# A GNN block on one core: the first columns of the adjacency built gather by gather, x loaded in three requests, a body of 80 first units

## The chip, the cores and the metric

The kernel runs on one core of a Trainium2 chip. The metric is the device time of one execution in microseconds (us).

## The reference

There are N = 1250 nodes with 512 features, and 21250 edges that come sorted by `dst`; each node has a loop edge. Two graph layers follow each other.

```python
agg = jax.ops.segment_sum(x[src], dst, num_segments=N)      # A^T x, A counts the edges
h = (1.0 + eps) * x + agg
h = relu(batch_norm(h @ W1 + b1, g1, be1))                   # 512 -> 1024
h = relu(batch_norm(h @ W2 + b2, g2, be2))                   # 1024 -> 512
x = layernorm(x + x + h)
h = relu(x @ lW1 + lb1) @ lW2 + lb2                          # 512 -> 256 -> 512
x = layernorm(x + h + segment_sum(h[src], dst, N))
```

## The kernel before

The sparse sum is turned into dense products. The kernel builds the count matrix AT (source nodes in 10 row tiles `k` of 128, destination nodes as 1250 columns) and multiplies x with it. As TensorE works exactly only on rounded operands, x is split into a rounded part `xh` and a rest `xl`; every unit of work of the aggregation, `aggregate(i, k)`, is therefore two passes over the columns of one chunk.

**The opening.** Each edge becomes one number, `pair` = dst * 1280 + src (L809). The numbers are stored to DRAM as `pairs` (ACT issues this, L561). A window is 10 destination nodes, and there are 125 windows, one for each partition. For each half window `c` (5 nodes) POOL gathers the run of 128 numbers that begins at its first edge (L472, two gathers, c = 0 and 1); the starts come from a count on TensorE and VectorE (L811 to L819, semaphores `rowsel`, `rowed`, `start_set`). VectorE subtracts each window's base (`rel`, L838), TensorE turns `rel` (L1182), and VectorE splits each number into a key and a low part (`keyT`, `loT`, L841 and L842, a pair of operations for each gather).

**Groups.** 25 groups of 5 windows each give 50 columns of AT. For a group, `one_hots(g)` (VectorE, L849 and L852) compares the low parts and the keys with a ramp, `build(g)` (TensorE, L1200) multiplies the two one-hot tiles into PSUM bank 0 or 1, and `group_out(g)` (ScalarE, L569) copies the counts to AT. The one-hot tiles have two buffers, so `one_hots(g)` waits for `build(g-2)`.

**Chunks and slots.** The columns are in chunks `CH` of 250, 500 and 500, which are complete after groups 5, 15 and 25 (`CHG`). Groups 0 to 4 are built in the opening, with filler products (`between`, L1176) on TensorE between them. After group 4 every engine reads a flag and takes the general body: slots g = 5 to 24, each with one `one_hots`, one `build`, one `group_out` and four aggregation units: slots 5 to 14 the 40 units of chunk 0, slots 15 to 24 the 40 units of chunk 1. The 40 units of chunk 2 follow behind slot 24 (`tail_units`). When a chunk's sum for feature tile `d` is complete (`h0_after`), VectorE adds the node's own features (`h0_own`, L863), ScalarE rounds it (`h0_high`), and VectorE takes the rest (`h0_low`, L870).

**x.** One request brings tiles 0 to 4 of x (`x_in`), a second and third, issued after both gathers were asked for (`runs_asked`), the others (`x_in2`). For each tile there are `x_cols(k)` (TensorE, four transposes, L1162), `x_turn(k)` (ScalarE, L577), `x_high(k)` (ScalarE, L565) and `x_low(k)` (VectorE, L828). For tiles 5 to 9 the tables `cols_at`, `turn_at`, `high_at` and `low_at` say in which slot each is done, at the slot's end.

Behind the aggregation stand the products with W1 (L1281) and W2 (L1298) and the second layer, which the change does not touch.

Of the kernel before, what the change touches and what calls it, by code (L numbers as in the profile page):

```python
# [14 lines left out]
P = 128  # L15
# [8 lines left out]
def gnn_kernel(nc, x, src, dst, eps, w1, b1, g1, be1, w2, b2, g2, be2, lw1, lb1, lw2, lb2, out, a_spill):  # L24
# [38 lines left out]
    with ctx:  # L63
# [122 lines left out]
        loT = misc("loT", [P, NW, 2], BF16)  # L186
        win_col, win_pair, ones, bounds = small(2), small(2), small(1), small(2)
# [66 lines left out]
        pads_set, bounds_set = sem("pads_set"), sem("bounds_set")  # L254
        rows_T, ln_var, ln_std_s, ln_aff, x1_last_set, x1_set = (
# [60 lines left out]
        def x_bank(k):  # L316
            return 3 + k if k < half else 6 + k % 2
# [18 lines left out]
        units = [(d, k) for k in range(NT) for d in range(DT)]  # L336
        units += [(c * DT + d, k) for c in range(1, len(CH)) for d in range(DT) for k in range(NT)]
        per = DT * NT
        slot_units = [[] for _ in range(NG)]
        for c in range(len(CH) - 1):  # L340
            slots = list(range(CHG[c], CHG[c + 1]))
            for j in range(per):
                slot_units[slots[j * len(slots) // per]].append(units[c * per + j])
        tail_units = units[(len(CH) - 1) * per:]
# [8 lines left out]
        assert EARLY == half and NT == half + 5 and max(cols_at) < CHG[1] and CHG[1] + HT <= NG and 2 + DT <= x_bank(half)  # L353

        def h0_after(g):
            return [i for i, k in slot_units[g] if k == NT - 1] if g >= 0 else []
# [80 lines left out]
        def _(pl):  # L437
# [116 lines left out]
        def _(act):  # L554

            act.dma_start(eps_in[:, :], eps.rearrange("(o d) -> o d", o=1).broadcast_to([P, 1])).then_inc(eps_in_s, 16)
            for r, (v, t) in enumerate(((b1, HT), (g1, HT), (be1, HT), (b2, DT), (g2, DT), (be2, DT))):
                r0 = r * HT if r < 3 else 3 * HT + (r - 3) * DT
                act.dma_start(par_r[r0:r0 + t, :], v.rearrange("(t p) -> t p", p=P)).then_inc(par_in, 16)
            act.wait_ge(pair_set, 1)  # L560
            act.dma_start(pairs.rearrange("(p f) -> p f", p=ER), pair[0:ER, :]).then_inc(pair_out, 16)  # L561

            def x_high(k):
                act.wait_ge(*((x_in, 16) if k < half else (x_in2, 32)))
                nc.scalar.activation(xh[0:rows[k], k, :], xs[0:rows[k], k, :], ACT.Copy).then_inc(xh_set, 1)  # L565

# [29 lines left out]
            for k in range(half):  # L596
                x_high(k)
            for k in range(half):
# [6 lines left out]
            for g in range(EARLY):  # L605
                group_out(g)
                if g in early_cols:
                    x_turn(early_cols[g])
# [187 lines left out]
        def _(v):  # L796
            n = [0]

            def link(ins):
# [7 lines left out]
            link(nc.vector.tensor_scalar(dst_f[0:ER, 0:EC], dst_i[0:ER, :], float(-BIG), None, ALU.add))  # L807
            v.wait_ge(src_in, 16)
            nc.vector.scalar_tensor_tensor(out=pair[0:ER, :], in0=dst_i[0:ER, :], scalar=float(STEP),  # L809
                                           in1=src_i[0:ER, :], op0=ALU.mult, op1=ALU.add).then_inc(pair_set, 1)  # L810
            link(nc.vector.tensor_scalar(below[0:ER, :], win_row[0:ER, :], dst_f[0:ER, EC - 1:EC], None, ALU.is_gt))  # L811
            nc.vector.scalar_tensor_tensor(out=edge_row[0:ER, :], in0=win_row[0:ER, :], scalar=dst_f[0:ER, 0:1],
                                           in1=below[0:ER, :], op0=ALU.is_gt, op1=ALU.subtract).then_inc(rowsel, 1)
# [7 lines left out]
            v.wait_ge(eps_in_s, 16)  # L821
            link(nc.vector.tensor_scalar(eps1[:, :], eps_in[:, :], 1.0, None, ALU.add))
            v.wait_ge(par_T, 1)
# [7 lines left out]
            for k in range(half):  # L831
                x_low(k)

            v.wait_ge(const, 4)
            for c in range(2):
# [3 lines left out]
                                        ALU.subtract, ALU.subtract).then_inc(rel_set, 1)  # L839
                v.wait_ge(rel_T, c + 1)  # L840
                link(nc.vector.tensor_scalar(keyT[:, :, c], ps[:, c, 0:NW], LIFT, LIFT, ALU.add, ALU.subtract))  # L841
                link(nc.vector.scalar_tensor_tensor(out=loT[:, :, c], in0=ps[:, c, 0:NW], scalar=P / 2 - 0.5,  # L842
                                                    in1=keyT[:, :, c], op0=ALU.add, op1=ALU.subtract))
# [30 lines left out]
            for g in range(EARLY):  # L874
                one_hots(g)
                if g == EARLY - 2:
                    v.wait_ge(counted, 1)
                    nc.vector.tensor_scalar(flag[0:1, :], ps[0:1, 2, 0:1], float(-2 * E), None,
                                            ALU.not_equal).then_inc(flag_set, 1)
            v.wait_ge(flag_set, 1)  # L880
            bad = v.value_load(flag[0:1, 0:1], min_val=0, max_val=1)
            with v.If(bad == 0):
# [539 lines left out]
```

## Time and profile before

| | |
|---|---|
| time, median of 3 | 250.22 us (249.56 to 250.61) |
| the profiled execution's own time | 249.95 us |
| its span | 248.1 us |
| TensorE busy with matmuls | 231.0 us, 93% of the span |
| VectorE busy | 156.2 us, 63% |
| ScalarE busy | 134.2 us, 54% |
| POOL busy | 88.0 us, 35% |
| chain that ended last: TensorE, VectorE, DMA, ScalarE | 70%, 12%, 7%, 6% |

The span runs from the first to the last instruction; 1.85 us of the execution's own time lie around it. The shares of busy time are averages over the whole kernel. What matters for the change is the first third: the opening up to the first aggregation unit, and the general body behind it. There the chain that ended last is read in order of time, with the timeline beside it.

### The profile page before, as it was taken

The page shows a single profiled execution, that of the slowest core. Times are in us where ns is not written, and L with a number is a line of the kernel's source. Part 1 is how long each engine was busy: PE and PEld are TensorE (multiplying, and loading weights), DVE is VectorE, ACT ScalarE, POOL GpSimd, SP SyncE. Part 2 cuts the span into 40 slices and gives each one's busy share as a digit, 9 for nine tenths or more (in the row PEclk, how much of TensorE's full clock was granted, in tenths as well). Part 3 has the DMA queues.
Part 4 walks back from the last instruction along what each step waited for, and adds up shares of the span by engine and source line. Part 5 has one row for each costly group of instructions (what it writes and reads, how often), then busy time and mean ns, then how long its engine had stood idle before and what let it go on. Part 6 is the DMA issues. An engine that isn't in the chain of part 4 may idle for free.

```text
span 248.1 us, 3897 instructions
## 1 busy us (share of the span) xinstructions
PE 231.0 (93%) x1454; PEld 197.3 (80%) x1454; DVE 156.2 (63%) x362; ACT 134.2 (54%) x233; POOL 88.0 (35%) x83
## 2 busy tenths in 40 slices
PE   0858999999999999999999999999999999999990
PEld 0845997777888888888888888888889997888970
DVE  1669899873966344555544316264876899796374
ACT  0656774763868067444455504457471639936373
POOL 5420000004920006565554500423456459701251
PEclk9999999999999999999999999999999999999998
DMA  3467800000066501111000087503209920000334
GB/s 100 156 214 214 202 0 3 1 3 3 3 261 239 198 1 45 42 42 45 0 0 0 4 206 142 106 3 60 45 4 170 202 85 3 0 0 0 131 127 160
DMA packets 32323, 19.96 MB, mean 80 GB/s; under 512 B 21927, under 2 KB 27084, under 8 KB 32302
## 3 DMA queue, kind: packets, MB, share of 16 engines
q1 hardware_dynamic: 31796, 19.45, 28.6%
q8 instruction: 13, 0.21, 0.4%
q0 software_dynamic: 160, 0.13, 0.2%
q10 hardware_dynamic: 346, 0.10, 0.2%
q14 instruction: 8, 0.07, 0.1%
HBM read 8.51 MB, written 5.92 MB: 58 GB/s over the span
## 4 chain that ended last, share of the span: by engine, by line
PE 70%; DVE 12%; DMA 7%; ACT 6%; issue 2%; POOL 1%; SPq 1%; DVEq 0%
PE ps L1281 22%; PE ps L1220 17%; PE ps L1298 11%; PE ps L1344 9%; PE ps L1362 6%; PE ps L1311 3%; DVE hot_s L849 3%; DMA plane_T<-planes 2%; PE ps L1200 2%; DMA src_i<-in_src 2%; DVE xT L984 2%; DMA pairs<-pair 2%; ACT planes L715 1%; DVE small_t L942 1%; DMA run<-pairs,start_i 1%
## 5 line engine op out<-in xcount | busy, mean ns | idle before, releaser
L942 DVE BATCH_NORM_STATS2 small_t<-ps 128x6 f32<-128x500 f32 (+1 forms) x36 | 21.6, 599 | 38.7 <-PE ps L1281 25.2
L1220 PE MATMUL ps<-AT,xh 128*128 128x500 f32 (+2 forms) x120 | 42.6, 366 | 0.4 <-ACT AT L569 0.4
L1220 PE MATMUL ps<-AT,xl 128*128 128x500 f32 (+2 forms) x120 | 40.9, 352 | 0.0
L1281 PE MATMUL ps<-h0h,wh 128*128 128x500 f32 (+1 forms) x96 | 33.9, 353 | 0.0
L1281 PE MATMUL ps<-h0h,wl 128*128 128x500 f32 (+1 forms) x96 | 33.9, 353 | 0.0
L1281 PE MATMUL ps<-h0l,wh 128*128 128x500 f32 (+1 forms) x96 | 33.8, 352 | 0.0
L485 POOL TENSOR_TENSOR wl<-w2s,wh 128x512 fp32r<-128x512 f32 x8 | 11.1, 1384 | 43.9 <-ACT wh L689 43.9
L480 POOL TENSOR_TENSOR wl<-w1s,wh 128x512 fp32r<-128x512 f32 x8 | 10.1, 1301 | 45.7 <-ACT AT L569 45.7
L1220 PEld LDWEIGHTS ps<-AT,xh 128*128 128x128 f32 (+1 forms) x120 | 22.6, 188 | 3.3 <-ACT AT L569 0.6
L1220 PEld LDWEIGHTS ps<-AT,xl 128*128 128x128 f32 (+1 forms) x120 | 22.7, 189 | 2.7
L1298 PE MATMUL ps<-a1h,wh 128*128 128x500 f32 (+1 forms) x96 | 23.7, 355 | 0.0
L1298 PE MATMUL ps<-a1h,wl 128*128 128x500 f32 (+1 forms) x96 | 23.5, 353 | 0.0
L1298 PE MATMUL ps<-a1l,wh 128*128 128x500 f32 (+1 forms) x96 | 23.4, 353 | 0.0
L569 ACT ACTIVATE AT<-ps 128x500 fp32r<-128x500 f32 x25 | 14.8, 590 | 15.6 <-PE ps L1200 15.6
L849 DVE TENSOR_TENSOR hot_s<-iota,loT 128x1280 bf16<-128x1280 bf16 x25 | 20.5, 820 | 2.3 <-PE ps L1200 2.2
L1344 PE MATMUL ps<-A,uh 128*128 128x512 f32 (+3 forms) x60 | 20.5, 357 | 0.0
L1281 PEld LDWEIGHTS ps<-h0h,wh 128*128 128x128 f32 x96 | 18.1, 188 | 2.9 <-issue 0.4
L1344 PE MATMUL ps<-A,ul 128*128 128x512 f32 (+3 forms) x60 | 20.3, 354 | 0.0
L1281 PEld LDWEIGHTS ps<-h0l,wh 128*128 128x128 f32 x96 | 18.0, 188 | 2.5
L1281 PEld LDWEIGHTS ps<-h0h,wl 128*128 128x128 f32 x96 | 18.0, 188 | 2.4
L489 POOL TENSOR_TENSOR a1l<-a,a1h 128x1250 fp32r<-128x1250 f32 x7 | 18.8, 2682 | 0.0
L663 ACT ACTIVATE small_t<-small_t 128x1 f32<-128x1 f32 x12 | 3.5, 295 | 27.7 <-DVE small_t L943 27.7
(148 smaller groups left out, 508.2 us busy)
## 6 DMA issues: line engine op xcount, KB each, us to landing
turns<-half_out SPq DMA_DIRECT2D x10, 320.0 KB, 2.2
out<-x SPq DMA_DIRECT2D x9, 256.0 KB
w1s<-in_L_gnn_W SPq DMA_DIRECT2D x4, 512.0 KB, 7.1
w2s<-in_L_gnn_W SPq DMA_DIRECT2D x8, 256.0 KB, 2.7
xs<-in_x SPq DMA_DIRECT2D x1, 1280.0 KB, 7.9
xs<-in_x SPq DMA_DIRECT2D x1, 1024.0 KB
lws<-in_L_gnn_W SPq DMA_DIRECT2D x1, 512.0 KB, 4.0
lw2s<-in_L_gnn_W SPq DMA_DIRECT2D x1, 512.0 KB, 4.2
```

Source lines behind the costliest of these rows:

```text
L480: nc.gpsimd.tensor_tensor(wl[:, t, :], w1s[:, t, :], wh[:, t, :].bitcast(F32), ALU.subtract).then_inc(w1l_set, 1)
L485: nc.gpsimd.tensor_tensor(wl[:, t, :], w2s[t % W2R][:, :], wh[:, t, :].bitcast(F32), ALU.subtract).then_inc(w2l_set, 1)
L489: nc.gpsimd.tensor_tensor(a1(a1l, t), a32[t % 2][:, :], a1(a1h, t).bitcast(F32), ALU.subtract).then_inc(a1l_set, 1)
L569: nc.scalar.activation(AT[:, :, g * WG * WIN:(g + 1) * WG * WIN].rearrange("p k (w d) -> p k w d", w=WG), ps[:, g % 2, 0:GCOLS].rearrange( ...
L849: nc.vector.tensor_tensor(hot_s[g % 2][:, :, :, :], iota2[:, None, :, :].broadcast_to([P, WG, P, 2]), loT[:, w, None, :].broadcast_to([P, ...
L942: link(nc.vector.bn_stats(stats[:, 6 * c:6 * c + 6], ps[:, zbank(t, c), 0:c1 - c0]))
L1220: last = mm(o, part[0:r, k, d * P:d * P + P], AT[0:r, k, c0:c1], start=(k == 0 and j == 0), stop=(k == NT - 1 and j == 1))
L1281: last = mm(ps[:, zbank(t, c), 0:c1 - c0], w[:, t, d * P:d * P + P], h[c][:, d, :], start=(d == 0 and j == 0), stop=(d == DT - 1 and j == 2))
L1298: last = mm(ps[:, zbank(t, c), 0:c1 - c0], w[:, k, (t - HT) * P:(t - HT + 1) * P], a1(a, k)[:, c0:c1], start=(k == 0 and j == 0), stop=(k ...
L1311: last = mm(u_at(k), x[:, d, P * k:P * k + r], w[:, d, :], start=(d == 0 and j == 0 and k % 2 == 0), stop=(d == DT - 1 and j == 2), skip_g ...
L1344: last = mm(v_at(i, m), (uh, ul)[j][0:r, k, m * P:m * P + P], a_rows(k)[0:r, c0:c1], start=(k == 0 and j == 0 and (m == 0 or v_banks[i][0] ...
L1362: last = mm(ps[0:r, y_banks[k % len(y_banks)], :], part[:, f:f + r], w[:, m, :], start=(m == 0 and j == 0), stop=(m == LT - 1 and j == 2))
```

## The change

- The count for the window starts is done ahead of `pair` on VectorE. ScalarE makes one small activation at its start, behind its parameter requests, and `runs_asked` waits for it (`table_set`).
- x comes in three requests: tiles 0 and 1 at once (`x_in`), tiles 2 to 4 after the first `rowed` (`x_mid`), tiles 5 to 9 after `runs_asked` as before. `x_cols(2)` stands ahead of everything of the gathers on TensorE.
- The first five groups are ordered by gather: groups 0 and 1 take the first halves of windows 0 to 19, group 2 the first halves of windows 20 to 24 and the second halves of windows 0 to 4, groups 3 and 4 the other second halves. Keys for these 25 windows are made apart for each gather (`early_keys`), those of the other 100 windows in one pair of operations (`late_keys`) behind the flag.
- In the general body `x_cols(6)` moves from the opening to slot 5; `x_low` of tiles 3 and 4 moves there too. Slots 5 to 14 hold all 40 units of chunk 0, now unevenly spread (7, 7, 6, 4, 4, 4, 2, 2, 2, 2), and 20 units more: feature tiles 0 and 1 of chunk 1 over its first 250 columns only. Slots 15 to 24 hold the other halves of these (20 units of 250 columns) and 20 whole units, four in each slot. Together these are 80 + 20 units, of 80 in the old count.

```diff
-        units = [(d, k) for k in range(NT) for d in range(DT)]
-        units += [(c * DT + d, k) for c in range(1, len(CH)) for d in range(DT) for k in range(NT)]
...
+        first = [(d, k, None) for k in range(NT) for d in range(DT)]
+        left = [(DT + d, k, 0) for k in range(NT) for d in range(SPLIT)]
+        second_units = [(DT + d, k, 1) for d in range(SPLIT) for k in range(NT)]
+        second_units += [(DT + d, k, None) for d in range(SPLIT, DT) for k in range(NT)]
+        first_per, left_per = [7, 7, 6, 4, 4, 4, 2, 2, 2, 2], [0] * 6 + [5] * 4
...
-        cols_at = {6: half + 2, 7: half + 3, 11: half + 4}
-        turn_at = {6: half + 2, 7: half + 3, 12: half + 4}
-        high_at = {5: half, 8: half + 1, 9: half + 2, 10: half + 3, 11: half + 4}
-        low_at = {7: half, 10: half + 1, 11: half + 2, 12: half + 3, 13: half + 4}
-        early_cols = {EARLY - 3: half, EARLY - 1: half + 1}
+        cols_at = {5: half + 1, 6: half + 2, 7: half + 3, 8: half + 4}
+        turn_at = dict(cols_at)
+        high_at = {5: half, 6: half + 1, 7: half + 2, 8: half + 3, 9: half + 4}
+        low_at = {5 + j: XA + 1 + j for j in range(NT - XA - 1)}
+        early_cols = {EARLY - 2: half}
...
-            sp.dma_start(xs[:, 0:half, :], x[0:half * P, :].rearrange("(t p) d -> p t d", p=P)).then_inc(x_in, 16)
+            sp.dma_start(xs[:, 0:XA, :], x[0:XA * P, :].rearrange("(t p) d -> p t d", p=P)).then_inc(x_in, 16)
+            sp.wait_ge(rowed, 1)
+            sp.dma_start(xs[:, XA:half, :], x[XA * P:half * P, :].rearrange("(t p) d -> p t d", p=P)).then_inc(x_mid, 16)
             sp.wait_ge(runs_asked, 1)
...
+            pl.wait_ge(table_set, 1)
             nc.gpsimd.memset(asked[0:1, :], 0.0).then_inc(runs_asked, 1)
...
+            act.wait_ge(const, 5)
+            nc.scalar.activation(asked[:, :], ones[:, :], ACT.Copy).then_inc(table_set, 1)
             act.wait_ge(pair_set, 1)
...
             v.wait_ge(eps_in_s, 16)
+            v.wait_ge(par_T, 1)
+            v.wait_ge(pair_out, 16)
...
+            def late_keys():
+                key, lo, turned_rel = keyT[:, WE:NW, :], loT[:, WE:NW, :], keys_at(0, 2, WE, NW)
+                nc.vector.tensor_scalar(key, turned_rel, LIFT, LIFT, ALU.add, ALU.subtract).then_inc(late_key, 1)
+                v.wait_ge(late_key, 1)
+                nc.vector.scalar_tensor_tensor(out=lo, in0=turned_rel, scalar=P / 2 - 0.5, in1=key,
+                                               op0=ALU.add, op1=ALU.subtract).then_inc(keys_read, 1)
...
-            for g in range(EARLY):
-                one_hots(g)
...
+            shifted(0)
+            x_low(XA)
+            early_keys(0)
+            early_hots(0)
+            shifted(1)
+            early_hots(1)
+            early_keys(1)
+            early_hots(2)
+            early_hots(3)
+            v.wait_ge(counted, 1)
...
+            early_hots(4)
...
-            for k in range(half):
+            for k in range(XA + 1):
                 x_cols(k)
...
-            for c in range(2):
-                pe.wait_ge(rel_set, c + 1)
-                nc.tensor.transpose(ps[:, c, 0:NW], rel[0:NW, c * RUN:(c + 1) * RUN], ident[0:NW, 0:NW]).then_inc(rel_T, 1)
-                between((4, 7)[c])
...
+            keys(0)
+            for k in range(XA + 1, half):
+                x_cols(k)
+            pe.wait_ge(xT_set, fill_bank - 2)
+            between(2)
+            build(0)
+            keys(1)
+            between(3)
+            build(1)
+            between(4)
+            build(2)
+            count()
+            between(4)
+            build(3)
+            x_cols(early_cols[3])
+            build(4)
```

## Rows read from the trace of the kernel before

**Rows 1.** Chain that ended last, opening: start us, us, engine or DMA, line.
```profile
1.15 4.40 DMA src_i<-in_src
...
6.02 3.88 DMA pairs<-pair
...
17.29 0.83 DVE hot_s L849
...
24.10 1.17 PE ps L1220 x8
```
**Rows 2.** Timeline of the opening: start us, us, engine, line, op, out<-in.
```profile
4.54 0.25 DVE L807 TENSOR_SCALAR dst_f<-dst_i 125x170 f32<-125x170 int32 x1 [4.54 <-DMA dst_i<-in_dst]
...
8.00 0.40 DVE L816 TENSOR_SCALAR_CACHE_REDUCE less<-ps,small_t 125x170 f32<-125x170 f32 x1 [1.24 <-PE ps L1154]
...
9.48 4.37 PE L1162 MATMUL ps<-ident,xs 128*128 128x128 f32 x20 [0.28 <-DMA xs<-in_x]
...
13.81 0.40 SPq L383 DMA_DIRECT2D xs<-in_x  x1
...
14.21 0.29 DVE L838 TENSOR_SCALAR rel<-run,small_t 125x128 f32<-125x128 f32 x1 [0.98 <-DMA run<-pairs,start_i]
...
15.91 0.29 DVE L838 TENSOR_SCALAR rel<-run,small_t 125x128 f32<-125x128 f32 x1 [0.29 <-DMA run<-pairs,start_i]
...
20.05 5.07 SPq L392 DMA_DIRECT2D w1s<-in_L_gnn_W  x4
```
**Rows 3.** Windows: length, busy of PE, PEld, DVE, ACT, POOL, PEclk, DMA share, GB/s.
```profile
6.00:7.00 1.00, 0.18 (x1) 0.18 (x2) 0.73 (x2) 0.68 (x1) 0.17 (x1) 1.00 1.06 400
...
9.00:10.00 1.00, 0.72 (x4) 0.58 (x5) 0.86 (x5) 0.54 (x2) 0.00 (x0) 1.00 0.08 18
```
**Rows 4.** DMA issues by line: KB each, us from issue to landing.
```profile
lws<-in_L_gnn_W SPq DMA_DIRECT2D x1, 512.0 KB, 4.0
...
turns<-half_out SPq DMA_DIRECT2D x10, 320.0 KB, 2.2
```
**Rows 5.** Chain that ended last, general body and what stands behind it.
```profile
26.82 0.44 PE ps L1162 x4
...
29.02 0.60 ACT xT L577
...
30.11 0.52 ACT xh L565
...
30.65 0.69 DVE xl L828
...
31.35 0.73 DVE hot_s L849
...
32.08 0.33 DVE hot_k L852
...
38.93 0.28 PE ps L1200 x10
...
39.20 1.91 PE ps L1220 x8
...
58.80 20.12 PE ps L1220 x88
...
78.92 54.96 PE ps L1281 x288
```
**Rows 6.** Timeline, passes over 250 columns in one slot, and a build that waited.
```profile
24.29 0.28 PE L1220 MATMUL ps<-AT,xl 128*128 128x250 f32 x1
...
25.00 0.28 PE L1220 MATMUL ps<-AT,xl 128*128 128x250 f32 x1
...
37.47 0.43 PE L1200 MATMUL ps<-hot_k,hot_s 128*128 128x50 bf16 x10 [0.22 <-DVE hot_k L852]
```
**Rows 7.** Groups by form, 0 to 80 us: busy us, mean ns, idle before.
```profile
L863 DVE SCALAR_TENSOR_TENSOR ps<-xT,small_t,ps 128x250 f32<-128x250 f32 x4 | 1.6, 476 | 0.0
...
L870 DVE TENSOR_TENSOR h0l<-ps,h0h 128x250 fp32r<-128x250 f32 x4 | 1.4, 410 | 0.0
```

More of the change, by code:

```diff
@@ L316, in x_bank, with x_landed, keys_at @@
         def x_bank(k):
-            return 3 + k if k < half else 6 + k % 2
+            return 3 + k if k < half else 5 if k == half else 6 + k % 2
+        fill_bank = 4
+        XA = 2
+        def x_landed(eng, k):
+            eng.wait_ge(*((x_in, 16) if k < XA else (x_mid, 16) if k < half else (x_in2, 32)))
+        def keys_at(c0, c1, w0, w1):
+            return ps[:, 2, P:P + 2 * NW].rearrange("p (c w) -> p w c", c=2)[:, w0:w1, c0:c1]
+        assert 3 * BT <= P and P + 2 * NW <= BANK
         assert NT % 2 == 0 and 2 * L <= BANK and NT // 2 <= 5 and half <= 5
@@ L333, in gnn_kernel @@
         NI = len(CH) * DT
-        units = [(d, k) for k in range(NT) for d in range(DT)]
-        units += [(c * DT + d, k) for c in range(1, len(CH)) for d in range(DT) for k in range(NT)]
-        per = DT * NT
-        slot_units = [[] for _ in range(NG)]
[L340 to L344, printed above, removed]
+        HALF_COLS = CH[0][1]
@@ new lines, in gnn_kernel @@
+        slot_units = [[] for _ in range(NG)]
+        for j in range(CHG[1] - CHG[0]):
+            a, b = sum(first_per[:j]), sum(left_per[:j])
+            slot_units[CHG[0] + j] = first[a:a + first_per[j]] + left[b:b + left_per[j]]
+        for j, u in enumerate(second_units):
+            slot_units[CHG[1] + j * (CHG[2] - CHG[1]) // len(second_units)].append(u)
+        assert sum(first_per) == len(first) and sum(left_per) == len(left) and len(CH) == 3
+        assert all(CHG[0] + j > HALF_READY for j, n in enumerate(left_per) if n)
@@ L563, in x_high, with early_out @@
             def x_high(k):
-                act.wait_ge(*((x_in, 16) if k < half else (x_in2, 32)))
+                x_landed(act, k)
                 nc.scalar.activation(xh[0:rows[k], k, :], xs[0:rows[k], k, :], ACT.Copy).then_inc(xh_set, 1)
+            def early_out(g):
+                act.wait_ge(built, g + 1)
+                for c, w0, w1, j in early_runs(g):
+                    last = nc.scalar.activation(
+                        AT[:, :, 0:CH[0][1]].rearrange("p k (w c d) -> p k w c d", c=2, d=SUB)[:, :, w0:w1, c, :],
+                        ps[:, g % 2, j * KEYS:(j + w1 - w0) * KEYS].rearrange("p (w d k) -> p k w d", d=SUB, k=NT),
+                        ACT.Copy)
+                last.then_inc(AT_set, 1)
             def group_out(g):
@@ L594, in h0_high @@
                 nc.scalar.activation(h0h[c][:, d, :], ps[:, 2 + i % 6, 0:c1 - c0], ACT.Copy).then_inc(h0h_set, 1)
-            for k in range(half):
+            for k in range(XA):
                 x_high(k)
-            for k in range(half):
+            for k in range(XA):
+                x_turn(k)
+            for k in range(XA, half):
+                x_high(k)
+            for k in range(XA, half):
                 x_turn(k)
@@ L829, in x_low, with shifted @@
                                         xh[0:rows[k], k, :].bitcast(F32), ALU.subtract).then_inc(xl_set, 1)
-            for k in range(half):
+            for k in range(XA):
                 x_low(k)
-            v.wait_ge(const, 4)
-            for c in range(2):
+            def shifted(c):
                 s = slice(c * RUN, (c + 1) * RUN)
@@ L882, in _ @@
             with v.If(bad == 0):
+                late_keys()
+                v.wait_ge(keys_read, 1)
                 for g in range(EARLY, NG):
@@ L1157, in x_cols @@
                 r = rows[k]
-                pe.wait_ge(*((x_in, 16) if k < half else (x_in2, 32)))
+                x_landed(pe, k)
                 if k >= half:
@@ L1214, in aggregate @@
                     else:
-                        pe.wait_ge(xT_set, half)
+                        pe.wait_ge(xT_set, half + 1 if 2 + i == x_bank(half) else half)
                 if i == 0:
                     pe.wait_ge(xl_set, k + 1)
+                    if k == 0 and keyed:
+                        pe.wait_ge(keys_read, 1)
                 r = rows[k]
                 for j, part in enumerate((xh, xl)):
-                    last = mm(o, part[0:r, k, d * P:d * P + P], AT[0:r, k, c0:c1], start=(k == 0 and j == 0),
-                              stop=(k == NT - 1 and j == 1))
-                if k == NT - 1:
+                    last = mm(o, part[0:r, k, d * P:d * P + P], AT[0:r, k, c0 + p0:c0 + p1],
+                              start=(k == 0 and j == 0 and h != 1), stop=(k == NT - 1 and j == 1),
+                              skip_group_check=(h is not None))
+                if k == NT - 1 and h != 0:
                     last.then_inc(h0_sum, 1)
-            for g in range(EARLY):
-                build(g)
-                if g == 0:
-                    count()
-                if g in early_cols:
-                    x_cols(early_cols[g])
-                elif g < EARLY - 1:
-                    between((2, 4, 4, 4)[g])
+            keys(0)
[14 more added lines that the diff above has]
+            build(4)
             pe.wait_ge(flag_set, 1)
@@ L1266, in _ @@
                 pe.wait_ge(AT_set, NG)
-                for u in units[0:(len(CH) - 1) * per]:
-                    aggregate(*u)
+                for u in first + [(DT + d, k, None) for d in range(DT) for k in range(NT)]:
+                    aggregate(*u, keyed=False)
             for u in tail_units:
```

78 lines of the change are left out of this document (54 added, 24 removed).

## The prediction

> **What bounds the kernel now.** I read the chain that ended last in order of time. Its first part is waiting and small work: src lands at 5.55, the pairs store takes 3.88 us, the one-hots begin at 17.29 and the first aggregation unit starts at 24.10 [rows 1]. From there TensorE is the chain almost without a break: slots of passes and builds, the tail of 88 passes in 20.12 us, and the W1 products from 78.92 [rows 5]. In the general body the chain leaves TensorE once, for x_turn, x_high, x_low and the one-hots, and a build waits 0.22 us [rows 5, 6]. So there are two accounts: when the first unit starts, and how long TensorE then needs to reach the W1 products, which is 78.92 - 24.10 = 54.82 us. Everything behind depends on that moment and moves with it.
>
> **Edit 1: x in three requests, and the order in the opening.** The store of pairs is issued at 6.02 and lands at 9.90 [rows 1]; in that time 1280 KB of x pass at 400 GB/s, until TensorE's wait for x ends at 9.48 [rows 2, 3]. Now only 512 KB are ahead of it; 768 KB less at 400 GB/s are 1.9 us, so x_in lands near 7.5 and the store's own data finds free engines. Bounds for the store: below, 2.2 us, the shortest kind of DRAM store here [rows 4], landing at 8.2; above, no gain, 9.9. I take 2.6 us, nearer the store of rows 4 since x_mid is issued only at about 6.8 (the three operations that end with edge_row begin at 4.54 and need some 1.1 us without the wait for src, and rowed comes 1.24 us behind them [rows 2]) and its data come more than 1 us later: P = 8.6. The activation that draws the table load forward lies in ScalarE's idle time; pair itself comes no earlier, as src lands when it did. Cost and gain there: nothing.
> By the Trainium skill, "DMA: Bandwidth & Descriptors", section "Why a DMA increments its semaphore by 16 and not by 1", a transfer over 125 partitions is spread over 5 engines only. By that rule part of the 3.88 us is the store's own and P would be near 9.2. The trace's fall from 400 to 18 GB/s by the window 9 to 10 doesn't decide it [rows 3].
> x_mid: 512 KB alone take 4.0 us [rows 4], 256 KB more at 400 GB/s 0.65: it lands at about 6.8 + 4.65 = 11.5. x_cols(2), now ahead of keys(0) on TensorE, ends by 12.4, at the pace of 0.87 us per tile (4.37 / 5 [rows 2]). The first rel is due after that, so it costs nothing; its cover is 0.5 us thick. x for tiles 5 to 9 took 20.05 - 13.81 = 6.2 us [rows 2]; issued at P + 4.4 = 13.0 less 0.2, it lands near 19, and x_cols(5) stands behind build(3), about 19.5. Covered.
>
> **Edit 2: gather by gather.** Before, all one-hots stood behind the second gather, whose rel began at 15.91, against 14.21 for the first [rows 2]. From the store's landing to the first rel are 14.21 - 9.90 = 4.3 us [rows 1, 2]. Then VectorE does rel (0.25), x_low(2) (0.69 [rows 5], which covers the turn) and the first keys: two operations on 25 columns, between 0.15 and 0.30 us each, with their waits 0.45. So the first one-hots begin at P + 5.7 = 14.3, against 17.29. Before, one-hots to first unit took 24.10 - 17.29 = 6.81 us [rows 1]; now rel(1) and keys(1) lie between them, 0.7 us more. First unit at P + 13.2 = 21.8. late_keys (two operations on 200 columns, about 0.4 each) end before build(4) is copied out, so keys_read costs nothing at slot 5.
> One charge remains. The transposes of tiles 0 to 4 ran at 0.218 us each, tile 6 at 0.11 [rows 2, 5]: the lower and the higher of the two clock levels (1.2 and 2.4 GHz), though the column of the granted clock reads 1.00 [rows 3]. Before, they ran from 9.48 without a break. Now TensorE idles ahead of x_cols(2) and ahead of keys(0), and x_cols(3), x_cols(4), the fillers and build(0) may run at the lower level: keys(1) comes 0.2 us late. First unit at 22.0: **2.1 us gained**.
>
> **Edit 3: the general body.** TensorE's work changes as follows.
> - x_cols(6), 0.44 us [rows 5], was done before the first unit and is now inside slot 5: +0.45.
> - Forty passes over 500 columns become 80 over 250. Six steps from 24.29 to 25.00 are 0.118 us each [rows 6]; a long pass is 20.12 / 88 = 0.2286 [rows 5]. 80 x 0.118 - 40 x 0.2286 = +0.3. Bounds: 0.1 (a slot's 1.91 us for eight long passes [rows 5] is 0.239 each) and 0.3.
> - Waits for one-hots. (a) Slots 5 to 8 are 24 units, 4 builds, 4 x_cols: 24 x 0.236 + 4 x 0.08 (start of each run of passes) + 4 x 0.28 + 4 x 0.45 = 8.9 us. At that point x_cols(9) releases x_turn, x_high, x_low(8), one_hots(11): 0.60 + 0.52 + 0.69 + 1.06 = 2.9 [rows 5], in all 11.8. TensorE comes to build(11) at 32 x 0.236 + 6 x 0.08 + 6 x 0.28 + 1.8 = 11.5: it waits 0.3. (b) Slots 15 to 19 are now short: 8 x 0.118 + 0.08 + 0.28 = 1.30 us each instead of 1.91 + 0.28 [rows 5], together 6.5. From slot 15's entry VectorE needs 0.45 for the build (0.43 [rows 6]), one_hots(17) 1.06, a wait of 0.25 for build(16), one_hots(18) 1.06, two h0_low of 0.35 (1.4 / 4 [rows 7]), one_hots(19) 1.06, two more h0_low, one h0_own of 500 columns (0.66, scaled from 0.40 [rows 7]), one_hots(20) 1.06: 7.0. TensorE waits 0.5. The old wait of 0.22 [rows 6] goes. Net +0.6.
> Together the body is +1.35 us longer, 56.2.
>
> **Sum.** -2.1 + 1.35 = -0.75 us at the start of the W1 products. Against the profiled execution (span 248.1, own time 249.95) this is 249.2; the median of the runs shown is 250.22, 0.27 above it, giving 249.5. I forecast 249.3.
>
> **Rivals.**
> 1. *The store waits for nothing that x did* (P = 9.7 instead of 8.6): x_mid takes the place of x, or the store's own time is long. For: 83 KB in short rows may be slow by themselves, and no row shows such a store alone. Against: 400 GB/s of x in the same time [rows 3]. The start gains 1.0 and the body loses 1.35: 250.3.
> 2. *The low clock outlasts the opening.* TensorE's work now has two gaps of 1 us or more ahead of the first build. If x_cols(5), the fillers and the five builds run at the lower level, build(3), x_cols(5) and build(4) queue behind the one-hots: the fillers and transposes of the last two steps double, 0.45 + 0.45 + 0.28 + 0.28 = 1.5 us late; and the first 2 us of the body at half pace cost 1.0. Time 249.3 + 2.4 = 251.7. It decides from the moment at which build(3)'s passes still run at half pace. The Trainium skill, "TensorE: Matmul & The Clock Gate", Part 1, has the lower level as the default which activity releases and idleness restores; by that rule this case is open, and no row before shows a gap of this kind.
> 3. *The body loses nothing by starvation*: the waits (a) and (b) vanish because VectorE is ahead, and the store lands at 8.2. Then -2.5 + 0.6: 248.1.
> 4. *x_mid late*: beyond 12 us each us of it delays keys(0) fully. Landing at 13 gives 250.3.
>
> **How the numbers follow.** Forecast 0.47 (248.7 to 250.1), rival 1 0.13, rival 2 0.11, rival 3 0.22, rival 4 0.07. The range reaches from rival 3 to short of rival 2: 248.0 to 251.0. About 0.5% (1.25 us) is what a measurement of this kernel can tell from no change. Faster than 248.97: rival 3 and a fifth of the forecast's range, 0.34; slower than 251.47: most of rival 2, 0.11; same 0.55.
>
> **What would show it.** Pairs landing near 8.6, the first rel near 12.9, first unit near 22.0, W1 products near 78.2, waits for one-hots at builds 11 and 20, and x_cols(3) at the lower level with the builds 2 to 4 at the higher. It is wrong if the store lands past 9.5, if keys(0) waits behind x_cols(2), if fillers before build(3) still run at half pace, or if something behind 78 us doesn't move with the start.

## The result, and the profile of the changed kernel

Medians of twelve executions of each kernel: 250.33 us before (249.56 to 250.75), 250.75 us after (250.41 to 251.14), a ratio of 1.0019 with the interval [1.0010, 1.0028]. The change costs 0.4 us where a gain of 0.9 was forecast; both lie within the 0.5% that the prediction counts as no change, but the interval excludes a gain. The profiled execution's span is 249.0 us against 248.1. (One of the five executions of e4, below, fell in a slow state, 291.66 us at a granted clock of 0.765, and is left out of its ratio.)

The chain that ended last, in order of time (start us, us, engine or DMA, line), answers to [rows 1] and [rows 5]:

```profile
0.72 4.13 DMA dst_i<-in_dst
...
7.26 5.08 DMA xs<-in_x
12.38 1.12 PE ps L1245 x4
...
14.51 0.83 DVE hot_s L911
...
22.04 1.86 PE ps L1310 x14
...
58.07 1.92 PE ps L1310 x8
60.02 0.74 DVE ps L936
60.76 0.59 DVE h0l L943
61.42 18.44 PE ps L1310 x80
79.86 54.94 PE ps L1380 x288
```

The first unit starts at 22.04 instead of 24.10: 2.06 us gained, as forecast (2.1). The W1 products start at 79.86 instead of 78.92: 0.94 us late. From there to the end of the span it is 169.1 us here and 169.2 before, so nothing behind this point takes part. All of the loss, 3.0 us from one mark to the other, lies in the general body: 79.86 - 22.04 = 57.82 us against 54.82. The forecast had allowed 56.2.

The timeline of TensorE shows which of its waits are new (start us, us, engine, line, op, tiles, and in brackets the idle time before it):

```profile
33.91 0.43 PE L1284 MATMUL ps<-hot_k,hot_s 128*128 128x50 bf16 x10 [0.21 <-DVE hot_k L925]
...
48.93 0.43 PE L1284 MATMUL ps<-hot_k,hot_s 128*128 128x50 bf16 x10 [0.40 <-DVE hot_k L925]
...
61.42 0.47 PE L1310 MATMUL ps<-AT,xh 128*128 128x500 f32 x1 [1.44 <-DVE h0l L943]
```

Builds 11 and 20 wait 0.21 and 0.40 us for their one-hots. The third wait was in no forecast: between the last pass of slot 24 and the first of the tail TensorE stands still for 1.44 us, where before it went on without a break (88 passes in one piece in [rows 5]; here the last 80 are a piece of their own). The trace puts it down to `h0_low` on VectorE (L943), which ended just before (the first of its two operations, 60.76 to 61.35 in the chain). The windows of 0.5 us show something else beside it (columns as in [rows 3]):

```profile
58.50:59.00 0.50, 0.50 (x4) 0.42 (x3) 0.00 (x0) 0.50 (x2) 0.22 (x1) 1.00 0.16 33
...
60.00:60.50 0.50, 0.00 (x0) 0.00 (x0) 0.48 (x1) 0.00 (x0) 0.50 (x2) 1.00 0.00 0
...
62.00:62.50 0.50, 0.50 (x4) 0.42 (x3) 0.50 (x2) 0.50 (x2) 0.50 (x1) 1.00 0.17 33
```

33 GB/s over 0.5 us are 16 KB. In this stretch no transfer of the kernel's own runs; the trace has the two packets, at 58.6 and 62.0, on a queue for instructions (window 57 to 64):

```profile
DMA packets 2, 0.03 MB, mean 5 GB/s; under 512 B 0, under 2 KB 0, under 8 KB 0
q8 instruction: 2, 0.03, 2.3%
```

The packets alone prove nothing: the kernel before has two as well, at 59.5 and 63.6, and TensorE works on through both (windows of the kernel before, same columns):

```profile
59.50:60.00 0.50, 0.50 (x4) 0.42 (x3) 0.00 (x0) 0.40 (x1) 0.49 (x1) 1.00 0.17 33
...
63.50:64.00 0.50, 0.50 (x4) 0.40 (x3) 0.50 (x1) 0.50 (x1) 0.50 (x1) 1.00 0.12 33
```

Behind slot 24 stands the end of the branch that every engine takes at the flag. The prediction looks only at this branch, the slots. There is a second one, for inputs whose edges do not fit the gathers: in TensorE's program it ends with 80 units of its own, unrolled (L1366), in both kernels. It never runs on this input, but it stands between slot 24 and the tail, and TensorE must jump over it. Counting instructions in the built program, two for each matmul (weight load and product), the jump stands at place 1007 before and lands at 1394; after the change, whose slots hold 20 units more, it stands at 1073 and lands at 1469.

So there were two theories. *The jump*: TensorE waits for instructions from the place where the jump lands. *The named wait*: the first tail unit waits for `h0_low`, because VectorE is late behind the new order of the sums. The second is what the trace says. The first rests on the place of the jump. The timeline of the kernel before already speaks against the second: there the tail's first pass starts before this `h0_low` does.

```profile
60.55 0.39 PE L1220 MATMUL ps<-AT,xh 128*128 128x500 f32 x1
...
61.40 1.43 DVE L870 TENSOR_TENSOR h0l<-ps,h0h 128x500 fp32r<-128x500 f32 x2
```

The timeline of the opening, for the steps of the forecast (start us, us, engine, line):

```profile
6.45 0.27 ACTq L596 DMA_DIRECT2D pairs<-pair  x1
...
7.26 0.40 SPq L412 DMA_DIRECT2D xs<-in_x  x1
...
9.59 1.41 POOL L503 DMA_INDIRECT run<-pairs,start_i  x1 [2.31 <-DMA pairs<-pair]
...
12.38 0.71 PEld L1245 LDWEIGHTS ps<-ident,xs 128*128 128x128 f32 x4 [2.39 <-DMA xs<-in_x]
...
13.15 0.29 DVE L886 TENSOR_SCALAR rel<-run,small_t 125x128 f32<-125x128 f32 x1 [2.17 <-DMA run<-pairs,start_i]
...
13.82 1.92 PE L1245 MATMUL ps<-ident,xs 128*128 128x128 f32 x8
...
15.95 0.62 PE L1284 MATMUL ps<-hot_k,hot_s 128*128 128x50 bf16 x10
...
18.53 0.44 PE L1284 MATMUL ps<-hot_k,hot_s 128*128 128x50 bf16 x10
```

The store of pairs lands at 9.3, 2.82 us after its issue, where it took 3.88 before [rows 1]. x_mid is issued at 7.26 and lands at 12.34, 5.08 us later; x_cols(2) starts with it.

### The profile page after: what moved, and what is told of

The parts are those of the page before. It is cut to its first block, busy times and chain, and to the rows that moved or that the text cites. A ratio compares the mean times of both kernels' runs of the same rounds, so it can differ in the third digit from the quotient of the medians.

```text
span 249.0 us, 3967 instructions
## 1 busy us (share of the span) xinstructions
PE 231.6 (93%) x1486; PEld 200.0 (80%) x1486; DVE 156.5 (63%) x364; ACT 134.5 (54%) x235; POOL 87.3 (35%) x83
## 4 chain that ended last, share of the span: by engine, by line
PE 82%; DVE 10%; DMA 4%; ACT 2%; issue 1%; DVEq 0%; ACTq 0%
PE ps L1397 22%; PE ps L1380 22%; PE ps L1310 16%; PE ps L1443 9%; PE ps L1461 6%; PE ps L1410 3%; DMA xs<-in_x 2%; PE ps L1284 2%; DMA dst_i<-in_dst 2%; DVE hot_s L922 2%; DVE hot_s L911 1%; PE ps L1245 1%; DVE h0l L943 1%; DVE small_t L1024 1%; ACT xr L706 1%; DVE hot_k L925 1%
## 5 line engine op out<-in xcount | busy, mean ns | idle before, releaser
L1310 PE MATMUL ps<-AT,xh 128*128 128x250 f32 (+3 forms) x140 | 44.5, 339 | 2.3 <-DVE h0l L943 1.4
L1310 PE MATMUL ps<-AT,xl 128*128 128x250 f32 (+3 forms) x140 | 42.7, 326 | 0.0
L1310 PEld LDWEIGHTS ps<-AT,xh 128*128 128x128 f32 (+1 forms) x140 | 26.4, 189 | 4.9 <-issue 1.8
L1310 PEld LDWEIGHTS ps<-AT,xl 128*128 128x128 f32 (+1 forms) x140 | 26.5, 189 | 2.1
L613 ACT ACTIVATE AT<-ps 128x500 fp32r<-128x500 f32 x20 | 11.9, 594 | 13.1 <-PE ps L1284 13.1
L1397 PEld LDWEIGHTS ps<-a1h,wh 128*128 128x128 f32 x96 | 15.9, 189 | 2.5
```

Source lines behind the costliest of these rows:

```text
L613: nc.scalar.activation(AT[:, :, g * WG * WIN:(g + 1) * WG * WIN].rearrange("p k (w d) -> p k w d", w=WG), ps[:, g % 2, 0:GCOLS].rearrange( ...
L1310: last = mm(o, part[0:r, k, d * P:d * P + P], AT[0:r, k, c0 + p0:c0 + p1], start=(k == 0 and j == 0 and h != 1), stop=(k == NT - 1 and j = ...
L1397: last = mm(ps[:, zbank(t, c), 0:c1 - c0], w[:, k, (t - HT) * P:(t - HT + 1) * P], a1(a, k)[:, c0:c1], start=(k == 0 and j == 0), stop=(k ...
```

## Experiments

**The length of the other branch.** Two kernels change only instructions that never run here.

```diff
 # e1_short_general, against the changed kernel
-                for u in first + [(DT + d, k, None) for d in range(DT) for k in range(NT)]:
+                for u in first:
 # e2_long_general, against the kernel before
-                for u in units[0:(len(CH) - 1) * per]:
+                for u in units[0:(len(CH) - 1) * per] + units[0:20]:
```

> The changed kernel, with one thing less: on TensorE the branch for general inputs, which these inputs never take, has 40 aggregation units instead of 80 (its general result would be wrong; nothing that is executed differs). The 1.44 us in which TensorE stands still behind slot 24 have two explanations. Theory J: TensorE jumps there over the general branch, and the instructions at the target have to be fetched first (a transfer of 16 KB on the instruction queue begins 1.4 us before the standstill). Then the shorter branch brings the target nearer, the standstill goes, the W1 products start near 78.4 instead of 79.86 and the time is 1.4 us below the changed kernel: 249.3, ratio to before 0.996. Theory H: the tail waits for h0_low on VectorE, as the profile names it. VectorE's program is the same, so the standstill stays at 1.4 us and the time at 250.75.

> The kernel before, with 20 dead aggregation units more in TensorE's branch for general inputs (84 instruction words that are jumped over and never executed). Theory J: the target of the jump moves from 387 to 471 words behind it, out of what is fetched ahead, so a standstill of 1 to 1.5 us appears behind slot 24 and the time rises from 250.33 to about 251.5 (ratio 1.005). Theory H: nothing that is executed changes, ratio 1.000.

e1: 248.99 us, ratio 0.9947 [0.9931, 0.9964], faster than the kernel before by 0.5%, and 1.8 us below the changed kernel's 250.75. It leaves 40 units out of the branch for other inputs, so it isn't a complete kernel. e2, which only adds dead instructions to the kernel before: 252.07 us, ratio 1.0063 [1.0046, 1.0080]. In the chain of e1 the tail is one piece again:

```profile
58.49 20.12 PE ps L1310 x88
```

and in the timeline of e2 the break is there, with `h0_low` named for it, in a kernel whose VectorE does what it did before:

```profile
62.58 0.47 PE L1220 MATMUL ps<-AT,xh 128*128 128x500 f32 x1 [1.37 <-DVE h0l L870]
```

From the first unit to the W1 products e1 takes 78.61 - 22.44 = 56.17 us (forecast for the change: 56.2) and e2 81.03 - 24.57 = 56.46 against 54.82. The break comes and goes with instructions that are never executed, by 1.65 us in each direction. The theory of the named wait falls. (The openings aren't equal even where the program is the same: e2's first unit comes 0.47 us later than in [rows 1]. At 20.7 a build takes 0.60 us and the transposes behind it 0.92 there, 0.43 and 0.64 in the kernel before: the lower clock level lasted longer. e1's comes 0.4 us later than the changed kernel's. So the time from first unit to W1 products is the measure of the body, and a difference of 0.4 us in one opening tells little.)

**The two branches in the other order.**

```diff
 # e3_swap, against the changed kernel; the branches change places, on TensorE alone
-            with pe.If(bad == 0):
-                for g in range(EARLY, NG):
...
-            with pe.Else():
+            with pe.If(bad != 0):
                 for k in cols_at.values():
...
+            with pe.Else():
+                for g in range(EARLY, NG):
```

> The changed kernel with the two branches in the other order in TensorE's program: the general branch first, the one taken behind it, so that TensorE jumps at the flag (where it waits for the last group anyway) and runs straight on behind slot 24. It computes the same for all inputs. Theory J: no standstill at the tail; the fetch now stands at the flag, read at about 20.5: if it takes the same time as at the tail (2.8 us from transfer to first pass) the first unit starts up to 1.3 us later than 22.04, so 249.3 to 250.6. Theory H: standstill unchanged, 250.75.

255.01 us, ratio 1.0178 [1.0149, 1.0207]. The break behind slot 24 is gone (the tail is one piece of 88), but a larger one stands ahead of the first unit. Timeline, and windows of 1 us with the granted clock in the column after the five engines:

```profile
26.38 0.55 PE L1310 MATMUL ps<-AT,xh 128*128 128x250 f32 x1 [5.12 <-issue]
```
```profile
25.00:26.00 1.00, 0.00 (x0) 0.00 (x0) 0.00 (x0) 0.00 (x0) 0.00 (x0) 0.80 1.19 311
26.00:27.00 1.00, 0.62 (x3) 0.66 (x4) 0.00 (x0) 0.00 (x0) 0.00 (x0) 0.50 1.20 296
```
```profile
26.38 3.32 PE ps L1310 x14
...
31.48 2.21 PE ps L1310 x14
```

5.12 us of standstill, some 4.2 more than the 0.89 at this place in the changed kernel, and then the price of the pause: the granted clock falls to 0.50, the lower of the two levels (1.2 GHz), and the first 14 passes take 3.32 us instead of 1.86. Body from first unit: 85.24 - 26.38 = 58.86 us, 2.7 more than e1's, which is the low clock: 1.46 and 0.50 us on the two stretches of 14 passes, 0.8 on the builds and transposes between them. By the Trainium skill, "TensorE: Matmul & The Clock Gate", Part 1, the lower level is what idleness brings back; the row agrees. Why this jump costs 4.2 us and the other 1.6 is taken up below the table.

**Whole units in the body.** The changed opening with 40 whole units of chunk 0 and 40 of chunk 1, four in each slot.

```diff
-        SPLIT = RING - DT
+        SPLIT = 0
-        first_per, left_per = [7, 7, 6, 4, 4, 4, 2, 2, 2, 2], [0] * 6 + [5] * 4
+        first_per, left_per = [4] * 10, [0] * 10
```

> The changed kernel with the old plan of units: slots 5 to 14 with four units of chunk 0 each, slots 15 to 24 with four whole units of chunk 1, no halves. All else as changed. My sum says that halving costs 0.3 us of passes and the uneven slots 0.6 us of waits, against some waits that the old plan has of its own while x_low of 7 tiles lies in slots 5 to 11 (VectorE 1.66 us a slot, TensorE 1.30 to 1.75). TensorE's program is 80 words shorter ahead of the jump: theory J lets the standstill go too. Together 249.3 to 250.0, with the first unit at 22.04 and no standstill. Theory H: standstill kept, about 250.7. If the uneven plan is what feeds TensorE, waits for one-hots of 1 us or more appear in slots 6 to 12.

249.44 us, ratio 0.9964 [0.9948, 0.9980]: a complete kernel, 0.4% faster than the kernel before and 0.5% below the changed one. Its timeline and chain:

```profile
22.14 0.35 PE L1310 MATMUL ps<-AT,xh 128*128 128x250 f32 x1 [0.90 <-ACT AT L605]
```
```profile
58.30 20.12 PE ps L1310 x88
78.42 54.95 PE ps L1380 x288
```

56.28 us from mark to mark, with four waits for one-hots (0.32, 0.16, 0.20 and 0.23) and no break. Against e1's 56.17 the halved units and the uneven plan bring 0.1 us; that is all they are worth, and in the changed kernel they cost 1.65. But e4's jump passes over as many instructions as the changed kernel's, 396: so it is not the length that decides. Only the place differs, by 80 instructions.

**The place of the jump.** These three settle that. Instructions that only wait for a semaphore raised long ago move everything behind them. Two such waits make one instruction: e9 has 160 waits on e4, e10 has 320 on the changed kernel, e11 has 80 on e4. Line numbers are higher by 3 in all three.

```diff
-            for k in range(XA + 1):
+            for k in range(XA):
                 x_cols(k)
+            for _ in range(160):
+                pe.wait_ge(rowsel, 1)
+            x_cols(XA)
```

> The kernel of whole units, with 80 more instructions on TensorE ahead of x_cols(2), each of which waits for a semaphore that has long been raised; they stand where TensorE waits 2.0 to 2.4 us for x_mid. No work is added. The distance of the jump over the general branch stays 396 instructions; the jump and its target move 80 places on, to places 1073 and 1469, where those of the changed kernel are. Theory P (a jump is free when its target lies in the 256-instruction block behind its own, and costs a standstill when it lies two blocks on): the standstill of about 1.4 us between slot 24 and the tail appears although this kernel runs slot 24 without it otherwise, so the time from the first unit to the W1 products grows from 56.3 to 57.6 to 57.8 us, and the time from 249.4 to about 250.8, plus what the waits cost in the opening (0 to 1 us). Theory D (the distance, or the work of the body, decides): no standstill, 56.3 us, time 249.4 plus the waits' cost.

> The changed kernel, with 160 more such instructions ahead of x_cols(2). The jump over the general branch moves from place 1073 to 1233, its target from 1469 to 1629, the distance stays 396. The runs so far put a block's border between 1394 and 1469, so the next lie between 1138 and 1213 and between 1650 and 1725: jump and target are then in neighbouring blocks. Theory P: no standstill between slot 24 and the tail; from the first unit to the W1 products 56.2 to 56.4 us instead of 57.8; the time is 250.75 - 1.4 = 249.3 plus what 160 waits cost in the opening (0 to 4 us, read from the start of x_cols(2), which was 12.38 in the changed kernel). Theory D: the standstill stays, 57.8 us.

> The kernel of whole units, with 40 more such instructions: the jump at place 1033, its target at 1429, between the places at which the target was free (1394) and cost (1469). Theory P: either no standstill (body 56.3 us, the border lies above 1429) or one of the full size, 1.3 to 1.5 us (body 57.7, the border lies below): nothing between. A rival in which the standstill grows with the distance that the fetch is behind would show a part of it, near half: 0.6 to 0.8 us.

Timeline of e9, and the chains of e10 and e11:

```profile
65.90 0.46 PE L1313 MATMUL ps<-AT,xh 128*128 128x500 f32 x1 [1.62 <-DVE h0l L943]
```
```profile
70.77 20.12 PE ps L1313 x88
```
```profile
58.29 20.12 PE ps L1313 x88
78.41 54.96 PE ps L1383 x288
```

| kernel | jump at | lands at | distance | first unit to W1 products | standstill at the tail |
|---|---|---|---|---|---|
| before | 1007 | 1394 | 387 | 54.82 us | none |
| changed | 1073 | 1469 | 396 | 57.82 | 1.44 us |
| e1 | 1073 | 1305 | 232 | 56.17 | none |
| e2 | 1007 | 1478 | 471 | 56.46 | 1.37 |
| e4 | 993 | 1389 | 396 | 56.28 | none |
| e9 | 1073 | 1469 | 396 | 58.14 | 1.62 |
| e10 | 1233 | 1629 | 396 | 56.16 | none |
| e11 | 1033 | 1429 | 396 | 56.36 | none |

All eight fit one rule. Let a border between blocks of 256 instructions lie between places 1429 and 1469, and others 256 to each side of it. Where the jump lands in the block behind its own, it costs nothing; where it lands two blocks on (changed, e2, e9), it costs 1.4 to 1.6 us of standstill and 1.64 to 1.86 in all (against e1, the kernel before and e4). e9 moves e4's body onto the changed kernel's places and gets its break; e10 moves the changed kernel's body off them and loses it; neither adds work to the body. There is nothing between none and all: e11, whose landing is 40 places short of e9's, pays nothing. The Trainium skill, "Runtime: NRT & Kernel Launch", section "Instruction fetch mechanics", has this rule: instructions come in blocks of 16 KiB, the next block in order is fetched ahead, and a taken branch that lands outside the two held forces a fetch before the engine goes on. The runs agree, and add the price. The same page gives TensorE room for 2048 instructions; were all of that filled ahead, none of these jumps would have to wait, and the measurements decide against it.

The rule has a rival. All three kernels that stand still land at 1469 or 1478, so "landing just behind a border costs" would fit the eight as well. The times of the 16 KB packets, held against the place that TensorE has reached, speak for the fetch. In every trace one packet begins for every 256 places or so that are passed (in the changed kernel's tail and behind it at 1692, 1947, 2250, 2458, 2709, 2986 and 3250), and one more at the jump. Counted in order, the block in which the jump lands comes, in the five kernels without the break, with a packet that begins 3.1 to 6.4 us ahead of the one at the jump. In the three with it, it comes only with the packet at the jump, and the first pass of the tail starts 2.80 us (changed), 2.73 (e2) and 2.99 (e9) after that packet's start. Which block a packet carries the trace doesn't say; this is a count.

e3 looks like an exception. There the conditional branch is taken at place 207 or so and lands at 603; with the borders above that is the neighbouring block, and it costs 4.2 us all the same. But by the same count the neighbouring block wasn't there yet. The first packet in the span begins, in all thirteen traces, only when TensorE has come to place 199 or later; in e3 it begins at 23.39, and the first unit follows it by 2.99 us, as at the tail in e9. So here too TensorE waits for a packet. Why this one begins as late as 23.39, when build 4 had started at 20.82, is open: x and W1 pass at 200 to 320 GB/s at that time, at the tail nothing does.

What these runs cost in total is another finding. e9 took 255.06 us (ratio 1.0194 [1.0169, 1.0218]) and e10 261.88 (1.0469 [1.0444, 1.0494]), far more than the 0 to 1 and 0 to 4 us allowed; e11 249.33. The chains of e9 and e10 have it:

```profile
12.33 4.54 issue
16.87 1.09 PE ps L1245 x4
```
```profile
12.41 13.07 issue
25.47 1.08 PE ps L1245 x4
```

x_cols(2) starts at 12.73 with 40 waiting instructions ahead of it (e11), at 16.87 with 80 and at 25.47 with 160: 4.14 us for 40 more and 8.60 for 80 more, 0.10 to 0.11 us each, although nothing had to be waited for. The 40 of e11 are hidden beneath x_mid, which lands at 12.59 there, with 78.41 for the W1 products as in e4. (x_cols(1) ends near 10.4 in all three. 40 at 0.10 us don't fit between that and 12.73, so TensorE's sequencer must have begun on them while the transposes still ran.)

**The opening.** Four kernels on e4, which has no break; its W1 products start at 78.42.

```diff
 # e5_no_hold: x_mid is asked for at once
-            sp.wait_ge(rowed, 1)
 # e8_hold_store: x_mid waits for the store of pairs
-            sp.wait_ge(rowed, 1)
+            sp.wait_ge(pair_out, 16)
 # e6_keys_first: x_cols(2) behind keys(0), x_low(2) behind early_hots(4)
-            for k in range(XA + 1):
+            for k in range(XA):
                 x_cols(k)
...
-            for k in range(XA + 1, half):
+            for k in range(XA, half):
                 x_cols(k)
 # e7_both_first: the first keys wait for both gathers
             x_low(XA)
+            v.wait_ge(run_in[1], 16)
             early_keys(0)
```

> All four kernels of this call stand on the one with whole units (e4: first unit at 22.14, no standstill, 249.44). Here x_mid no longer waits for rowed: tiles 2 to 4 of x are asked for right behind tiles 0 and 1, as in the kernel before. My term for the store said that x was what made it 3.88 us; then it is 3.5 to 3.9 us again and ends near 10, the first rel comes 0.6 us later, but x_mid lands by 9.7 and keys(0) no longer queues behind x_cols(2): first unit 22.5, time 249.8. Rival: the store's time is its own (2.9 us with or without x), then only the queue behind x_cols(2) changes, first unit 21.6 to 22.0, time 249.2.

> x_mid waits until the store of pairs has landed: nothing but the store moves in those microseconds. It prices the store alone. If x_mid, asked for at 7.26, still slows the store, it lands in 2.2 to 2.6 us instead of 2.85; if 2.85 is its own time it stays. x_mid lands near 14.4 instead of 12.4 and holds keys(0) behind x_cols(2) for about 2 us: first unit near 24, time 251.3. This also shows what a late x_mid costs.

e5: 250.20 us, ratio 0.9998 [0.9987, 1.0009]; e8, one execution: 250.01. The chain of e5, of e8, and e8's first `rel` in its timeline:

```profile
6.23 3.94 DMA pairs<-pair
...
79.33 54.94 PE ps L1379 x288
```
```profile
6.38 2.31 DMA pairs<-pair
8.71 4.43 DMA xs<-in_x
...
79.07 54.96 PE ps L1380 x288
```
```profile
13.88 0.29 DVE L886 TENSOR_SCALAR rel<-run,small_t 125x128 f32<-125x128 f32 x1 [3.49 <-DMA run<-pairs,start_i]
```

With all of x in flight the store takes 3.94 us, with x_mid asked for after `rowed` 2.82 in the changed kernel (2.49 to 2.85 over the nine kernels that ask so), alone 2.31. So x slows it by up to 1.6 us, and holding x_mid back is worth 79.33 - 78.42 = 0.9 us, which the two medians bear out (250.20 and 249.44). Holding it longer wins another 0.4 to 0.5 us on the store and loses it again: x_mid then passes during the gathers, and the first `rel` comes 3.46 us after its gather is described, against 2.15 in the changed kernel (2.05 to 2.84 over the nine). That x_mid is what delays the gather is argued from this, not shown apart. e8's W1 products are 0.65 us behind e4's, in one execution: of the three positions the change's middle one is the best here.

> x_cols(2) and x_low(2) are taken out of the way of the first keys: x_cols(2) behind keys(0) on TensorE, x_low(2) behind the fifth group's one-hots on VectorE. In the changed kernel x_mid landed at 12.34 and x_cols(2) ended at 13.5, at the edge of rel's end (13.44). If this queue is what sets keys(0), the first one-hots start 0.3 to 0.6 us earlier than 14.59, the first unit at about 21.7, and the 0.6 us of x_low(2) come back in part as waits for one-hots: 249.1. If the gather sets it, the first one-hots move by 0.1 or less and the time is 249.4 to 249.9, as x_low(2) now lies on VectorE's chain.

> VectorE waits for the second gather before it makes the first keys: the building gather by gather is undone, everything else stays. By my sum the first keys could start 1.7 us (15.91 - 14.21) after the first rel's start in the kernel before; the second gather is now described in 1.2 us instead of 1.3, so about 1.5 us after 13.15, against 0.9 us at which keys(0) start now: 0.6 to 0.8 us later, first unit at 22.8, time 250.1. If the gain of building by gather is hidden anyway, 249.4.

e6: 250.68 us, ratio 1.0016 [1.0004, 1.0028]; e7: 249.73, 0.9984 [0.9971, 0.9996]. W1 products:

```profile
79.67 54.95 PE ps L1380 x288
```
```profile
78.72 54.96 PE ps L1381 x288
```

e6 loses 1.25 us. `keys(0)` starts 0.43 us behind the start of `rel` with x_cols(2) ahead of it or without, so nothing is won there, but three tiles' transposes then stand between keys(0) and keys(1), at the lower clock level, and keys(1) runs at 17.19 instead of 16.48. Of the 1.25 us, 0.73 lie ahead of the first unit (22.87 for 22.14) and 0.52 in the body (56.80 for 56.28); the edit moved x_low(2) too, and the two moves weren't taken apart. e7 says what it is worth that keys of the first gather do not wait for the second: 0.3 us, no more than two equal openings differ by, and its interval overlaps e4's.

So neither half of the idea explains the 2 us by itself. In e5 the store lands at 10.17, later than the 9.90 before, and its first unit still starts at 22.97, 1.13 us earlier than before. The faster store is worth 22.97 - 22.14 = 0.8, gather by gather 22.37 - 22.14 = 0.2, and about 1 us of the gain is neither. POOL's two gathers are described in 1.41 + 1.21 us instead of 1.88 + 1.30, which is half of it; what made them shorter, and where the other half lies, isn't shown.

## Why the prediction was wrong

**The start of the body: right, partly by cancelling errors.** First unit forecast at 22.0, measured 22.04. VectorE had dst at 4.87 instead of 4.54, and the store was issued at 6.45 instead of 6.02; it took 2.82 us for the 2.6 assumed: P = 9.3 for 8.6. The later issue had been put at nothing; `pair` now stands behind edge_row on VectorE and begins at 6.08 instead of 5.65. Against that the gather was described in 1.41 us (1.88 before) and the first `rel` came 3.88 us after the landing, not 4.3: 13.15 for 12.9. One-hots began at 14.51 (14.3). From there to the first unit 7.53 us (7.7). x_mid landed at 12.34, for 11.5: with 5.1 us against 4.65, and issued 0.45 later. The 0.5 us of cover named for it was used up almost to the end: x_cols(2) ended at 13.50 and keys(0) started at 13.58, as soon as `rel` was there; e6 shows that the wait for it cost nothing.

**Rival 1** (the store waits for nothing that x did) is answered by e5 and e8: x is worth 1.6 us of the 3.9. What is left alone is 2.31 us, close to the shortest store of [rows 4]. The landing at 9.3 is near the 9.2 that the prediction gives by the Trainium skill's rule of 5 engines ("DMA: Bandwidth & Descriptors"), but that is luck: 0.4 us of it is the later issue and some 0.5 us is x_mid. That 5 engines serve the store fits the traces, where its semaphore gets five updates from DMA engines up to the landing.

**Rival 2** (the low clock outlasts the opening) did not come. x_cols(3) and x_cols(4) took 1.92 us for 8 and builds 0 and 1 0.62 us each, at the lower level; from build(2) at 18.53 it is 0.44, and the body's passes are at the higher one. That is the course that the forecast had assumed, with keys(1) late. e3 shows what the rival would have cost, had the gap been long enough: 1.46 us on the first 14 passes alone.

**Rivals 3 and 4.** Rival 3 did not come: the store landed at 9.3 and not 8.2, and both waits for one-hots are there. For rival 4 x_mid landed at 12.34, past its 12 (12.97 in e1), and keys(0) was not held up: it starts 0.43 us behind the start of `rel` in both, as `rel` was late too.

**The body's own terms: right in sum.** Without the jump the body takes 56.17 us for 56.2. Builds 11 and 20 wait 0.21 and 0.40 us (0.3 and 0.5), less the old 0.22 a net of 0.4 for the 0.6; the passes and transposes then cost 0.95 for the 0.75, so two small errors cancel.

**The step that failed** is the sum of the body, "Together the body is +1.35 us longer, 56.2": it counts passes, builds, transposes and waits, and takes the step from slot 24 to the tail to be free because it was free in the kernel before. It was free there by 75 places at most (by at least 36, as e11's landing at 1429 is free): the jump landed at 1394, and the border lies before 1469. The change adds 20 units, 80 instructions, to the branch that runs; with fewer ahead of it the landing moves by 75 places, over the border. The missing term is 57.82 - 56.17 = 1.65 us. With it the forecast of 249.3 is 250.95; 250.75 was measured. None of the rivals held it, and rival 3, in which the body loses less than forecast, got 0.22 where the body lost more. The list of what would show the prediction wrong did not name it either: it looked for waits on semaphores, and this is a wait for none.

## What to carry to other kernels

A branch that is never taken still costs if it stands between a jump and where the jump lands; when a change lengthens unrolled code on either side, look at the places of the two, and measure the same kernel with dead code cut to size. A standstill of an engine whose named releaser does nothing new is a suspect: change instructions that don't run, and see whether it moves. And when two transfers compete, check what the one held back runs into next: in e8 the store gained 0.4 us and the gather behind it lost 1.3 (3.46 us for 2.15).

## What the runs showed of the hardware

- A taken jump of TensorE cost nothing when it landed in the next block of 256 instructions, and 1.4 to 1.6 us of standstill when it landed two blocks on, whatever its length (396 in both cases). The trace names a semaphore's releaser for it.
- TensorE's instructions came in packets of 16 KB, one for every 256 places or so. Where it stood still at a jump, it went on 2.7 to 3.0 us after the start of a packet that began at the jump (changed, e2, e9). Packets near the jump without a standstill are in the other traces too.
- The conditional jump ahead of the body in e3 cost 4.2 us over the usual wait: the program's first packet began only at 23.39, and the first pass came 2.99 us after it. Why so late is open.
- An instruction that only waits for a semaphore long raised cost TensorE 0.10 to 0.11 us.
- A store of 83 KB over 125 partitions took 2.31 us alone (one execution), 2.49 to 2.85 with 768 KB asked for 0.7 to 0.8 us behind it, and 3.94 with 1280 KB ahead of it.
- After 5.1 us of idleness the granted clock read 0.80 and then 0.50, and passes over 250 columns ran at about half pace for 3.3 us. In the opening the column read 1.00 while transposes and builds ran at the lower level (builds 0.62 us against 0.44).
